# Graph network over 16 batches on one core: the last two parts of the neighbour sums moved ahead of slot 1's gates

## The reference, cut to what matters

```python
adj_norm = adj / (jnp.sum(adj, axis=-1, keepdims=True) + 1e-08)
h_neigh = jnp.einsum('bnm,bmf->bnf', adj_norm, x)
x1 = layernorm(x + relu(concat([x, h_neigh]) @ weight + bias))

A = (adj != 0).astype(x.dtype)
h = x1
for l in range(5):
    agg = jnp.einsum('bij,bid->bjd', A, h @ weight[l])
    r, z = sigmoid(i_r + h_r), sigmoid(i_z + h_z)   # i_* from agg, h_* from h
    h = (1 - z) * tanh(i_n + r * h_n) + z * h
out = layernorm(x1 + h * mask)
```

## Time and profile before

| | |
|---|---|
| median of 3 runs | 608.36 us (607.6 to 609.06) |
| profiled execution | 605.41 us |
| its span, first to last instruction | 603.6 us |
| granted TensorE clock, mean | 0.992 |
| PE, PEld busy | 97%, 77% |
| DVE, ACT, POOL busy | 87%, 68%, 72% |

### The profile page before, as it was taken

One profiled execution on the slowest core, in us unless ns is written; L12 is line 12 of the kernel. 1 busy time (PEld: TensorE's weight loads), 2 busy tenths in 40 slices (PEclk: granted clock), 3 DMA queues, 4 the chain that ended last, 5 costly groups with the idle time before them and its releaser, 6 DMA issues.

```text
span 603.6 us, 9825 instructions
## 1 busy us (share of the span) xinstructions
PE 582.8 (97%) x2633; PEld 467.0 (77%) x2633; DVE 522.2 (87%) x1141; ACT 408.6 (68%) x812; POOL 433.8 (72%) x347
## 2 busy tenths in 40 slices
PE   7999999999999999999999999999999999998992
PEld 6678788777778787878888787788878888786771
DVE  5986978988888998989899898989989898967677
ACT  5767674767858677786767777676877777664451
POOL 0645463957959889796978879697987969666343
PEclk9999999999999999999999999999999999999996
DMA  8703105336374563737365373736537373211101
GB/s 273 296 27 126 44 32 174 120 112 226 107 242 119 186 191 110 244 115 249 109 195 183 110 249 115 240 115 203 167 131 246 110 235 110 74 36 35 36 2 52
DMA packets 92005, 86.70 MB, mean 144 GB/s; under 512 B 7760, under 2 KB 64080, under 8 KB 91984
## 3 DMA queue, kind: packets, MB, share of 16 engines
q1 hardware_dynamic: 91712, 86.31, 44.0%
q10 hardware_dynamic: 272, 0.13, 0.1%
HBM read 62.56 MB, written 23.86 MB: 143 GB/s over the span
## 4 chain that ended last, share of the span: by engine, by line
PE 80%; DVE 9%; issue 3%; ACT 3%; DMA 2%; POOL 2%; SPq 0%; POOLq 0%; DVEq 0%; ACTq 0%
PE ps_tok L1583 11%; PE ps_tok L1576 10%; PE ps_r L1408 5%; PE ps_r L1410 5%; PE ps_r L1409 5%; PE ps_z L1408 5%; PE ps_z L1410 5%; PE ps_z L1409 5%; PE ps_in L1408 3%; PE ps_in L1410 3%; PE ps_in L1409 3%; PE ps_b L1408 2%; PE ps_b L1410 2%; PE ps_b L1409 2%; PE ps_hn L1410 2%
## 5 line engine op out<-in xcount | busy, mean ns | idle before, releaser
L749 POOL TENSOR_TENSOR z_h<-z_gate,h 128x512 f32<-128x512 f32 x80 | 110.2, 1378 | 16.0 <-ACT z_gate L967 16.0
L675 POOL TENSOR_TENSOR h_lo<-h,h_hi 128x512 fp32r<-128x512 f32 x64 | 83.9, 1311 | 46.4 <-ACT h_hi L771 46.4
L878 ACT ACTIVATE ps_in<-ps_in,gru_bias 128x512 f32<-128x512 f32 x80 | 53.0, 662 | 79.6 <-DVE ps_in L1250 79.3
L1576 PE MATMUL ps_tok<-edges,tok_hi 128*128 (+1 forms) x320 | 88.4, 398 | 3.6 <-DVE tok_lo L993 2.7
L668 POOL TENSOR_TENSOR tok_lo<-rows,tok_hi 128x512 fp32r<-128x512 f32 x48 | 67.3, 1401 | 32.7 <-ACT tok_hi L771 32.7
L1583 PE MATMUL ps_tok<-edges,tok_lo 128*128 (+1 forms) x320 | 88.2, 397 | 0.3 <-POOL tok_lo L668 0.3
L1380 DVE SCALAR_TENSOR_TENSOR r_hn<-ps_hn,gru_bias,r_gate 128x512 f32<-128x512 f32 x80 | 59.3, 742 | 28.6 <-ACT r_gate L956 27.5
L657 POOL TENSOR_TENSOR adjt_lo<-adjt_in,adjt_hi 128x512 fp32r<-128x512 f32 x56 | 77.4, 1395 | 2.3 <-ACT adjt_hi L771 2.3
L1576 PEld LDWEIGHTS ps_tok<-edges,tok_hi 128*128 128x128 f32 x320 | 59.3, 188 | 19.6 <-DVE tok_lo L993 3.4
L1583 PEld LDWEIGHTS ps_tok<-edges,tok_lo 128*128 128x128 f32 x320 | 59.2, 188 | 16.7 <-POOL tok_lo L668 2.2
L1294 DVE SCALAR_TENSOR_TENSOR ps_in<-z_gate,ps_in 128x512 f32<-128x512 f32 x80 | 55.4, 692 | 13.4 <-ACT ps_in L878 11.6
(11 more groups left out here) (187 smaller groups left out, 1575.4 us busy)
## 6 DMA issues: line engine op xcount, KB each, us to landing
adjt_in<-in_adj_t_dram SPq DMA_DIRECT2D x14, 1024.0 KB, 5.6
adj_in<-in_adj_dram SPq DMA_DIRECT2D x14, 1024.0 KB, 7.8
rows<-passage SPq DMA_DIRECT2D x192, 64.0 KB, 2.0
passage<-early_blocks SPq DMA_DIRECT2D x36, 256.0 KB, 2.2
x_in<-in_x_dram SPq DMA_DIRECT2D x16, 256.0 KB, 8.0
xt_in<-in_x_t_dram SPq DMA_DIRECT2D x15, 256.0 KB, 3.1
out_dram<-y_out SPq DMA_DIRECT2D x15, 256.0 KB, 8.1
passage<-last_blocks SPq DMA_DIRECT2D x14, 256.0 KB, 2.2
```

What stands on the lines that cost most here:

```text
L675: nc.gpsimd.tensor_tensor(h_lo[new][:], h[new][:], raw(h_hi[new][:]), ALU.subtract).then_inc(s_h_lo, 1)
L749: nc.gpsimd.tensor_tensor(z_h[:], z_gate[:], h[own][:], ALU.mult).then_inc(s_zh, 1)
L1576: nc.tensor.matmul(ps_tok[:], tok_hi[:, c * P:(c + 1) * P], edges_from(c, unit[0]), start=c == 0, stop=False)
```

## The change

The six products of parts 2 and 3 are issued between slot 1's state products and its gates in all windows that prepare a batch, by `neighbour_sums`, which the earlier windows already use. Part by part means: wait for `adjt_lo` of the part, then its three products. `last_neighbour_sums` is gone. Number and shapes of all instructions are as before, on every engine.

```diff
-            def last_neighbour_sums(made):
-
-                for j in (2, 3):
-                    nc.tensor.matmul(ps_b[2][:], y_hi[:, j, :], adjt_hi[:, j, :], start=False, stop=False)
-                    nc.tensor.matmul(ps_b[2][:], y_lo[:, j, :], adjt_hi[:, j, :], start=False, stop=False)
-                for j in (2, 3):
-                    pe.wait_ge(s_adjt_lo, made + j + 1)
-                    last = nc.tensor.matmul(ps_b[2][:], y_hi[:, j, :], adjt_lo[:, j, :], start=False, stop=j == 3)
-                return last
-
...
-                        if slot == 1 and not w.means():
+                        if slot == 1:
                             pe.wait_ge(s_own, w.prepared(2, 2))
                             neighbour_sums((2, 3), w.prepared(C, 0)).then_inc(s_nsum, 1)
                     if unit:
...
                         if slot == 4 and w.means():
                             first_state()
-                        if slot == 1 and w.means():
-                            pe.wait_ge(s_own, w.prepared(2, 2))
-                            last_neighbour_sums(w.prepared(C, 0)).then_inc(s_nsum, 1)
                         if w.first > 0 or slot > 0:
                             pe.wait_ge(s_h, w.units(slot))
```

## The result

The changed kernel takes 622.01 us in the median of 4 runs (621.82 to 623.4), the kernel before 607.99 in that comparison. The ratio is 1.0238, with a 95% interval of 1.0216 to 1.0261: 14 us slower. The forecast was 624.1 us, with a range of 619 to 627.5.

What follows compares the result with a forecast made beforehand. PE, busy 97% of the span, was taken to bound the kernel. 15.9 us over 11 windows plus 0.2 in window 3 gave 16.1, cut to 15.7 for waits given back; 608.4 + 15.7 = 624.1 us, range 619 to 627.5.

Steps and rivals of the forecast that it cites:

- The wait: Slot 1, parts 2 and 3: PE idles for GpSimd's adjt_lo, 1.45 us in window 7, plus 0.11 for an uneven second product.
- That it recurs: PE's stall at adjt_lo in slot 1 comes again in each window from 4 to 14, about 1.45 us each.
- the ring: Dependency loop: slot 1's r sigmoid, state, passage, mean rows, x1, h, GpSimd's 14 us, adjt_lo 3, back to that sigmoid.
- Rival 1: One stall, then GpSimd is ahead and later stalls vanish: 1.5 to 2 us in all, 610 us; chance 6%.
- rival 2: Half hidden, as PE really holds some link: 0.5 to 1.0 us a window, 614 to 619.4 us; chance 12%.
- rivals 3 and 5: 3: faster, slot 2's agg_lo wait goes, 605.8 us, 2%; 5: no change, for instance an earlier count, 1%.
- 11 x 1.45 = 15.9: Lateness of slot 1's r sigmoid, 1.45 us in each of 11 windows, 4 to 14: 15.9 us in all.
- Window 3's 0.2: In window 3 slot 1's r sigmoid would be only 0.2 us later, bringing the sum to 16.1 us.
- No step of that chain waits for PE now ... The change closes it: The chain from slot 1's r sigmoid to adjt_lo 3 was open; putting the r gate behind adjt_lo 3 closes it.
- What is given back: Slot 2's r gate stops waiting for agg_lo (0.13 and 0.11 us in window 7); total taken as 15.7, not 16.1.
- Clock: PE's granted clock stays at its upper level, as after a 2.75 us idle time between 546 and 552 us; nothing counted.
- rival 4: The clock falls to 1.2 GHz after each stall, 3 us in each of 11 windows: 657 us; chance 3%.

Runs made afterwards that it cites:

- New place, parts sooner: Changed kernel with GpSimd's slot 0 h_lo (1.26 us) moved behind adjt_lo 3 in windows 2 to 14: 608.20 us, kernel before beside it 607.36.
- one more copy: Changed kernel with an extra ScalarE copy of transposed x1 ahead of the copy starting GpSimd's run: 628.19 us; same edit in the kernel before: 612.80 us.

## Why the prediction was right, and where it was not

*The wait* was right in place and cause and close in size: in window 7, 1.25 us by starts and 0.2 for two uneven products, where 1.45 and 0.11 were forecast. *That it recurs* was right. The pitch rose by 1.41 us. New place, parts sooner (1.25 less for 1.26 us taken out of GpSimd's run) and one more copy in the changed kernel (0.50 more for 0.48 us put ahead of it) change it by what their edits take or give. Those are the ring's links on ScalarE's copies and on GpSimd; the links through the passage and `x1` are read from the waits, and no experiment touches them. Rival 1 (one stall) and rival 2 (half hidden) fall by the same numbers, rivals 3 and 5 by the time.

*The sum* was 1.7 us too large: 15.7 forecast, 14.0 measured. The term that was mis-sized is "11 x 1.45 = 15.9". The r sigmoid of window 14 is late by 523.48 - 509.13 = 14.35 us, that of window 4 by 1.41. Nine of the ten steps between add 1.41 in the mean, but window 5 adds only 0.24: before, ScalarE's `tok_hi` in window 4 waited 2.69 us for its rows from DRAM, after 1.36, and starts at nearly the same time. In the changed kernel:

```profile
171.96 0.63 ACT L771 ACTIVATE tok_hi<-rows 128x512 fp32r<-128x512 f32 x1 [1.36 <-DMA rows<-passage]
```

In the kernel before it started at 171.87. SyncE's issues ahead of it, the store of the sums and the first load of them, which waits for the store to land, in the kernel before:

```profile
161.24 0.43 SPq L558 DMA_DIRECT2D mean_passage<-late_blocks  x1
164.45 1.73 SPq L564 DMA_DIRECT2D mean_t<-mean_passage  x4
```

and in the changed kernel:

```profile
162.58 0.34 SPq L558 DMA_DIRECT2D mean_passage<-late_blocks  x1
164.60 1.73 SPq L564 DMA_DIRECT2D mean_t<-mean_passage  x4
```

So a slow transfer in the kernel before, 3.2 instead of 2.0 us, took in most of the delay of one window. This is read from the traces; no experiment tries it, and why it was slow is open. It isn't one bad execution: in window 4 the same distance is 3.1 to 3.6 us in five more of the profiled kernels, and in the other six, where it is 2.0 to 2.3, SyncE's issue just ahead of the store took 2.6 to 3.0 us instead of 1.7. The kernel before shows it in its own pitch: 36.08 us from window 4 to window 5, and 34.8 to 35.1 in every later step. I had read the ring in window 7 and multiplied it, without looking for a window in which something else is later. Window 3's 0.2 did not come either (123.35 against 123.41).

*"No step of that chain waits for PE now ... The change closes it"* failed. The copy added to the kernel before shows that the ring was already all but closed, through `tok_lo` of slot 1, with 0.2 us of slack. The change did not create it but moved its way back to PE from `tok_lo` to `adjt_lo` 3, further down GpSimd's run. The forecast survived because the ring's length was taken from the rows as a whole.

*What is given back* failed: slot 2's wait did not go, but in window 14. In window 7 of the changed kernel:

```profile
273.94 0.39 PE L1410 MATMUL ps_z<-h_hi,whh_lo 128*128 128x512 f32 x1
274.26 0.50 PE L1408 MATMUL ps_r<-agg_hi,wc_hi 128*128 128x512 f32 x1
274.59 0.39 PE L1409 MATMUL ps_r<-agg_lo,wc_hi 128*128 128x512 f32 x1
```

It loses 0.09 + 0.10 us by starts. PE and the others seem to be late by the same amount, so that their distance stays; no experiment tries this. The 0.4 us that the forecast took off its 16.1 for this brought it nearer to the measured time by luck.

*Clock*: in the loop it held, 1.00 from 233 to 523 us of the changed kernel, so rival 4 fell; behind the loop it did not, as below. The ground that was given, one idle time of 2.75 us that had left the clock as it was, was luck of that execution.

## What to carry to other kernels

Before moving work ahead on a saturated engine, find when its latest operand is made, on the engine that makes it, and follow that engine's run back to what starts it. If this leads round to the place of the move, the wait recurs in every turn, however much idle time the maker has; and the cure is the maker's order, here one operation of 1.26 us that nobody needed yet. Look in the same run for the operation with the least slack, for it tells how near the ring is to pacing the kernel already, and look at more than one turn before multiplying.

## What was not expected of the hardware

The kernel has one idle time of PE of 2.74 to 2.75 us behind the loop (551.54 in the kernel before, in the stretch of the earlier trace rows), the same in all twelve profiled kernels. In three of them, the one before among them, the clock stayed at 1.00 behind it. In nine it fell to its lower level. The changed kernel is one of these. Busy time and granted clock around it, and the products that follow:

```profile
563.00:574.00 11.00, 8.27 (x26) 6.56 (x27) 6.04 (x17) 2.75 (x6) 4.73 (x5) 0.69 0.14 37
```

```profile
565.73 2.07 PE L1566 MATMUL ps_tok<-edges,tok_hi 128*128 128x512 f32 x4 [2.75 <-DVE tok_lo L993]
...
569.30 0.63 PE L1408 MATMUL ps_hn<-h_hi,whh_hi 128*128 128x512 f32 x1
569.73 0.63 PE L1409 MATMUL ps_hn<-h_lo,whh_hi 128*128 128x512 f32 x1
...
572.14 0.39 PE L1409 MATMUL ps_z<-h_lo,whh_hi 128*128 128x512 f32 x1
572.37 0.39 PE L1410 MATMUL ps_z<-h_hi,whh_lo 128*128 128x512 f32 x1
```

Products at the lower level, 1.2 GHz, are 0.43 us apart, as in the earlier trace rows, and 0.23 again afterwards. From slot 1's r sigmoid in window 14 to the end of the span are 94.5 to 94.6 us in the three profiles without the fall and 95.4 to 96.5 in the nine with it, 96.5 in the changed kernel. So the two profiles differ by 620.0 - 603.6 = 16.4 us, of which 2.0 are this and not the change, while the medians differ by 14.0. A forecast made against one profiled execution should ask which of such chances that execution had. The Trainium skill, "TensorE: Matmul & The Clock Gate", section "HAM oscillation — how this bites in real kernels", ties the lower clock to idle times of PE; these traces agree that it follows one, and show that the same idle time does it in some executions only.
